# Six more tasks of a gelu stage moved into attention's last unit, and one relu half's additions moved behind its last tile

## What is computed

```python
x = x + 0.5 * gelu_mixture(layernorm(x))      # a: 8 experts, 128 -> 512 -> 128, the best 2 by router
x = x + attention(layernorm(x))               # b: 16 heads of 8, causal, rotary positions
x = x + 0.5 * gelu_mixture(layernorm(x))      # c: as a
x = x + 0.5 * relu_mixture(layernorm(x))      # d: 8 experts, 128 -> 256 -> 128, the best 1 by router
x = x + selective_scan(layernorm(x))          # e: 64 states, chunks of 64 steps
x = x + 0.5 * relu_mixture(layernorm(x))      # f: as d
```

## Time and profile before

| | us |
|---|---|
| median of 3 runs | 1462.83 |
| lowest and highest of them | 1460.21, 1464.10 |
| the profiled execution's own time | 1457.12 |
| its span, first to last instruction | 1455.0 |
| around the span | 2.12 |
| mean granted clock of PE over the span | 0.866 of full |
| busy in the span: PE, DVE, ACT, POOL | 1125.1, 971.6, 771.4, 747.8 |

### The profile page before, as it was taken

The page is one execution under the profiler, slowest core; times in us unless marked ns, Lnnn a source line. Parts: engine busy times, 40 slices in busy tenths (PEclk is TensorE's granted clock), DMA queues, the critical chain, the costliest instruction groups (busy, mean ns, idle before and its releaser), DMA issues.

```text
span 1455.0 us, 26867 instructions
## 1 busy us (share of the span) xinstructions
PE 1125.1 (77%) x9744; PEld 715.4 (49%) x9744; DVE 971.6 (67%) x2128; ACT 771.4 (53%) x1515; POOL 747.8 (51%) x658
## 2 busy tenths in 40 slices
PE   2869999758888888778899978816578888885784
PEld 1646767402222222355677655613466666664463
DVE  5887676677777777288766663355468888886332
ACT  2666667404666566667667733315655666651231
POOL 4774566573333331167466563525167888882322
PEclk9999999957999999889999988957578989985796
DMA  6110000031111120010000001210411111101122
GB/s 204 58 44 1 1 1 1 0 58 30 30 30 30 30 30 1 1 58 31 29 1 1 0 12 55 72 36 15 154 47 39 39 36 35 41 19 61 55 79 62
DMA packets 90601, 55.39 MB, mean 38 GB/s; under 512 B 54236, under 2 KB 83684, under 8 KB 89575
## 3 DMA queue, kind: packets, MB, share of 16 engines
q1 hardware_dynamic: 88423, 49.48, 12.9%
q0 software_dynamic: 2048, 4.20, 1.0%
HBM read 31.06 MB, written 14.20 MB: 31 GB/s over the span
## 4 chain that ended last, share of the span: by engine, by line
PE 42%; DVE 23%; issue 14%; ACT 13%; POOL 3%; SPq 2%; DMA 2%; POOLq 0%; DVEq 0%; ACTq 0%
PE ps L700 13%; PE ps L841 4%; PE ps L871 4%; DVE arena L1858 4%; PE ps L982 4%; DVE xn L1642 2%; ACT hr L1149 2%; PE ps L954 2%; DVE maxima L1861 2%; ACT arena L1249 2%; DVE arena L1929 2%; ACT arena L1149 2%; PE ps L809 2%; PE ps L793 2%; PE ps L769 1%
## 5 line engine op out<-in xcount | busy, mean ns | idle before, releaser
L1529 POOL TENSOR_TENSOR arena<-arena 128x512 f32<-128x512 f32 x126 | 214.8, 1724 | 86.4 <-ACT arena L1249 37.2
L700 PE MATMUL ps<-xp,wup 128*128 128x512 f32 x768 | 206.8, 415 | 13.1 <-ACT hr L1149 9.6
L1553 POOL TENSOR_TENSOR hr<-arena,hr 128x512 fp32r<-128x512 f32 x128 | 171.8, 1348 | 85.9 <-ACT hr L1149 85.9
L700 PE MATMUL ps<-hr,wdn 128*128 128x512 f32 x768 | 200.4, 411 | 3.8 <-issue 2.7
L1249 ACT ACTIVATE arena<-ps 128x512 f32<-128x512 f32 x256 | 143.2, 597 | 107.5 <-PE ps L954 101.4
L1149 ACT ACTIVATE arena<-ps 128x512 f32<-128x512 f32 x256 | 163.4, 638 | 61.7 <-PE ps L700 61.4
L1205 ACT ACTIVATE arena<-ps 128x1024 f32<-128x1024 f32 (+1 forms) x192 | 148.3, 810 | 79.6 <-PE ps L856 78.3
L1794 DVE TENSOR_TENSOR hr<-arena,hr 128x512 fp32r<-128x512 f32 x128 | 126.2, 997 | 87.8 <-ACT hr L1149 86.8
L700 PEld LDWEIGHTS ps<-xp,wup 128*128 128x128 f32 x768 | 146.5, 198 | 62.5 <-POOL wup L1540 16.8
L1929 DVE TENSOR_TENSOR arena<-arena,ps 128x1024 f32<-128x1024 f32 x189 | 154.1, 856 | 17.2 <-PE ps L967 16.9
L1149 ACT ACTIVATE hr<-ps 128x512 fp32r<-128x512 f32 x256 | 165.5, 646 | 0.0
(11 more groups left out here) (240 smaller groups left out, 1876.6 us busy)
## 6 DMA issues: line engine op xcount, KB each, us to landing
arena<-up_dram SPq DMA_DIRECT2D x16, 256.0 KB, 2.9
arena<-dn_dram SPq DMA_DIRECT2D x16, 256.0 KB, 3.1
ys_rows<-arena SPq DMA_DIRECT2D x8, 320.0 KB, 2.5
arena<-up_dram SPq DMA_DIRECT2D x2, 1024.0 KB, 4.8
arena<-dn_dram SPq DMA_DIRECT2D x2, 1024.0 KB, 6.9
arena<-xs_rows SPq DMA_DIRECT2D x4, 512.0 KB, 4.8
b_parts<-arena SPq DMA_DIRECT2D x1, 1536.0 KB, 5.0
dt_parts<-arena SPq DMA_DIRECT2D x1, 1536.0 KB, 6.4
```

The lines of the kernel that those rows point to most:

```text
L700: mm = e.matmul(out, left(a), right(b), start=(first and n == 0), stop=(last and n == 2))
L1529: e.tensor_tensor(hsf[t % 3][:, cols], decayf[u % 2][:, t4 * W + cols.start:t4 * W + cols.stop], hsf[(t - 1) % 3][:, cols], ALU.mult).then ...
L1553: e.tensor_tensor(hr[:, ex % 2, 1, fc, :], hid[:, ex % 2, fc, :], hr[:, ex % 2, 0, fc, :], ALU.subtract).then_inc(MX["rest_pool"], 1)
```

## The change

It does three things.

1. `early_tasks` grows from 3 tasks to 9: besides `stats` 0, `norm` 0 and `stats` 1 it now has `turn` 0, `logits` 0, `logits back` 0, `shift` 0, `norm` 1 and `route` 0 of stage c. They stand in the last unit ahead of steps 5 (`stats` 0, `norm` 0), 6 (`turn` 0), 7 (`logits` 0, `stats` 1), 8 (`logits back` 0), 9 (`shift` 0), 10 (`norm` 1) and 11 (`route` 0). Before stage c's first expert only `stats` 2 is left.
2. These tasks use PSUM banks 0 and 1 in the place of 6 and 7, with waits for the projection's additions (`proj_added`) and for the last split of heads (`unit_split`), and the projection of block 2 waits for the shift (`shifted`). `rot` moves to the end of attention's pieces, so that `xp` lies on it and not on pieces that the last unit still uses.
3. In the relu stages all 8 additions of the first half, and in stage d the scan's tasks behind them, go to the last step of the loop, s = 32.

```diff
--- before.py
+++ after.py
@@ -206,8 +206,6 @@
         qkf = carve(NT * 2 * D)
         qk = qkf.rearrange("p (i c d) -> p i c d", c=2, d=D)
         probT = qkf.rearrange("p (s h q) -> p s h q", s=2, h=HG)
-        rot = carve(2 * T + P)
-        rotv = rot[:, 0:2 * T].rearrange("p (c i d) -> p c i d", c=2, d=D)
         vflat = carve(T + P)
         vall = vflat[:, 0:T].rearrange("p (i d) -> p i d", d=D)
         ctxv = xn[:]
@@ -223,6 +221,8 @@
         masked_s = [qzf[:, n * S + 4 * P:n * S + 8 * P] for n in (2, 3)]
         vpad = carve(2 * ST_ * HG * 32).rearrange("p (s i h c) -> p s i h c", s=2, i=ST_, h=HG)
         oT = carve(2 * 512).rearrange("p (a q) -> p a q", a=2)
+        rot = carve(2 * T + P)
+        rotv = rot[:, 0:2 * T].rearrange("p (c i d) -> p c i d", c=2, d=D)
         assert top[0] <= kept
 
         top[0] = 0
@@ -367,9 +367,9 @@
                 before = [t(w, g) for g in range(NTB // B) for w in tasks_of(st)] + [t(w, 0) for w in ROUTED] + \
                          [t(w, g) for g in range(NTB // B, NTB) for w in tasks_of(st)] + [t(w, 1) for w in ROUTED]
             along = {5: [t("rweights", 0), t("rweights", 1)]}
-            along.update({NTL + 11 + n: [t("add", 2 * n), t("add", 2 * n + 1)] for n in range(HT // 2)})
+            along[B * NTL + 2] = [t("add", n) for n in range(HT)]
             if nxt:
-                along.update({NTL + 11 + HT // 2 + n: [(nxt, w, g) for w in tasks_of(nxt)] for n, g in enumerate(range(NTB // B))})
+                along[B * NTL + 2] += [(nxt, w, g) for g in range(NTB // B) for w in tasks_of(nxt)]
             return before, along
 
         AT = {k: sem(f"att_{k}") for k in (
@@ -437,11 +437,17 @@
 
         EARLY = NTB - NTB // B
         after = [stages[n + 1] for n, st in enumerate(stages[:-1]) if st["kind"] == "attention"]
-        early_tasks = [(after[0], "stats", 0), (after[0], "norm", 0), (after[0], "stats", 1)] if after else []
+        early_tasks = [(after[0], w, g) for w, g in (
+            ("stats", 0), ("norm", 0), ("turn", 0), ("logits", 0), ("stats", 1), ("logits back", 0), ("shift", 0),
+            ("norm", 1), ("route", 0))] if after else []
+
+        def task_bank(st, what, g):
+
+            return (0 if what == "turn" else 1) if (st, what, g) in early_tasks else (6 if what == "turn" else 7)
 
         def last():
             extra = {1: [("ctx", 0, 0)], 2: [("ctx", 0, 1), ("proj", 0, 0)], 3: [("proj", 0, 1)],
-                     **{5 + n: [("task", 0, n)] for n in range(len(early_tasks))}}
+                     **{4 + n: [("task", 0, k) for k in m] for n, m in enumerate(((0, 1), (2,), (3, 4), (5,), (6,), (7,), (8,)))}}
             m = -1
             for what, k, n in order(True, False):
                 if what == "st" and n % 2 == 0:
@@ -640,21 +646,25 @@
                 e.wait_ge(LN["xn_ready"], st["norm"] + g + 1)
                 if not (isinstance(n, int) and n == 0):
                     e.wait_ge(LN["xnT_ready"], n)
+                bank = task_bank(st, what, g)
+                if bank == 0:
+                    e.wait_ge(AT["proj_added"], NTB // B)
                 for j in range(TPB):
                     at = xn_flat[:, bass.ds(xn_at(st, g) + j * P, P)]
-                    mm = e.transpose(ps[:, 6, j * P:(j + 1) * P], at, ident[:])
+                    mm = e.transpose(ps[:, bank, j * P:(j + 1) * P], at, ident[:])
                 mm.then_inc(LN["tp_done"], 1)
             elif what == "logits":
                 n = st["route"] + g
                 e.wait_ge(LN["xnT_ready"], st["turn"] + g + 1)
                 if not (isinstance(n, int) and n == 0):
                     e.wait_ge(LN["shifted"], n)
-                e.matmul(ps[0:E, 7, :], rw[st["kind"]][:], xnT[:, bass.ts(g, TB)], start=True, stop=True
+                e.matmul(ps[0:E, task_bank(st, what, g), :], rw[st["kind"]][:], xnT[:, bass.ts(g, TB)], start=True, stop=True
                          ).then_inc(LN["logitsT_done"], 1)
             elif what == "logits back":
                 e.wait_ge(LN["logitsT_ready"], st["route"] + g + 1)
+                bank = task_bank(st, what, g)
                 for j in range(TPB):
-                    mm = e.matmul(ps[:, 7, j * E:(j + 1) * E], logitsT[:, j * P:(j + 1) * P], ident[0:E, 0:E],
+                    mm = e.matmul(ps[:, bank, j * E:(j + 1) * E], logitsT[:, j * P:(j + 1) * P], ident[0:E, 0:E],
                                   start=True, stop=True)
                 mm.then_inc(LN["logits_done"], 1)
             elif what == "rlogits":
@@ -922,6 +932,8 @@
             e.wait_ge(AT["o_normed"], 2 * NU + 2)
             for g in range(EARLY, NTB):
                 e.wait_ge(AT["proj_added"], g - 1)
+                if g == EARLY:
+                    e.wait_ge(LN["shifted"], after[0]["route"] + 1)
                 context(e, g)
             for g in range(EARLY, NTB):
                 project(e, g, 2 + g)
@@ -1116,12 +1128,15 @@
                 e.activation(std[:, 0:TPB], veps[:, 0:TPB], ACT.Sqrt).then_inc(LN["std_ready"], 1)
             elif what == "turn":
                 e.wait_ge(LN["tp_done"], st["turn"] + g + 1)
+                bank = task_bank(st, what, g)
+                if bank == 0:
+                    e.wait_ge(AT["unit_split"], 2 * NU)
                 if st["kind"] == 0:
-                    e.copy(xp[:, 0, bass.ts(g, TB)], ps[:, 6, :])
-                e.copy(xnT[:, bass.ts(g, TB)], ps[:, 6, :]).then_inc(LN["xnT_ready"], 1)
+                    e.copy(xp[:, 0, bass.ts(g, TB)], ps[:, bank, :])
+                e.copy(xnT[:, bass.ts(g, TB)], ps[:, bank, :]).then_inc(LN["xnT_ready"], 1)
             elif what == "logits":
                 e.wait_ge(LN["logitsT_done"], st["route"] + g + 1)
-                e.copy(logitsT[:], ps[0:E, 7, :]).then_inc(LN["logitsT_ready"], 1)
+                e.copy(logitsT[:], ps[0:E, task_bank(st, what, g), :]).then_inc(LN["logitsT_ready"], 1)
             elif what == "shift":
                 e.wait_ge(LN["shifted"], st["route"] + g + 1)
                 e.activation(lg[:], lg[:], ACT.Exp).then_inc(LN["exp_done"], 1)
@@ -1644,6 +1659,8 @@
                     ins.then_inc(LN["xn_ready"], 1)
                 elif what == "logits" and st["kind"] == 0:
 
+                    if task_bank(st, what, g) == 1:
+                        e.wait_ge(AT["unit_split"], 2 * NU)
                     e.wait_ge(LN["xnT_ready"], st["turn"] + g + 1)
                     cols = bass.ts(g, TB)
                     e.tensor_tensor(xp[:, 1, cols], xnT[:, cols], xp[:, 0, cols], ALU.subtract).then_inc(LN["rest_ready"], 1)
@@ -1652,7 +1669,7 @@
                     kind = st["kind"]
                     l = lg[:]
                     e.wait_ge(LN["logits_done"], st["route"] + g + 1)
-                    e.tensor_tensor(l, ps[:, 7, 0:TPB * E].rearrange("p (i e) -> p i e", e=E),
+                    e.tensor_tensor(l, ps[:, task_bank(st, what, g), 0:TPB * E].rearrange("p (i e) -> p i e", e=E),
                                     rb[kind][:].unsqueeze(1).to_broadcast([P, TPB, E]), ALU.add).then_inc(LN["route_step"], 1)
                     e.wait_ge(LN["route_step"], n + 1)
                     e.tensor_reduce(rowmax[:], l, AX.X, ALU.max).then_inc(LN["route_step"], 1)
```

## The result

| | before | changed |
|---|---|---|
| median of 15 runs, us | 1461.09 | 1449.08 |
| lowest and highest | 1456.82, 1477.89 | 1441.31, 1460.64 |
| profiled execution: its time, span | 1457.12, 1455.0 | 1449.86, 1448.1 |

The ratio of the times is **0.994, with a 95% interval of 0.9921 to 0.996**: faster by 0.6%, or 8.8 us (5.8 to 11.5). The forecast was a gain of 8.7 us, a median of 1454.1. The profiled executions differ by 7.3 us.

What follows compares the result with a forecast made beforehand. No single engine was taken to bound the span (PE 42% of the chain, DVE 23%). Gains of 4.4, 4.05 and 0.3 us sum to 8.7, so 1462.83 - 8.7 = 1454.1 us, range 1449.8 to 1460.2.

Steps and rivals of the forecast that it cites:

- Part 1a: Attention's last unit: the added copies and handovers lengthen it on ACT by 1.9 us, bounds 1.2 to 4.
- Part 1b: Start of stage c: no wait on `comb`, slow first up products, fast second; expert 2 starts 4.4 us earlier.
- rival B: PE keeps its clock over attention's closing transposes and projection: part 1 gives 6.5, 11 in all, 1451.8 us; chance 0.14.
- The late ranking costs twice: Stage c: PE waits 5.39 us for the split of `comb`, then expert 1's up products take 5.33, not 3.02.
- Part 2: End of stage d: the loop's last two steps take 2.88 us in place of 6.93, a gain of 4.05.
- Part 3: First half's additions leave the relu loops: a gain of 0.2 us in stage d and 0.1 in f.
- The 2.19 at f's end: Stage f's moved additions lie under 13.48 idle us; without that cover they would cost 2.19 us.
- Rival D: Reordered code brings new stalls of mean 4.9 us at three places: 6.0 us slower, 1468.8 us; chance 0.04.
- The median of the runs is 5.71 above that execution: Base of the forecast: 1462.83 us for the kernel before, against its profiled execution of 1457.12.

Runs made afterwards that it cites:

- attn_only: The changed kernel with the relu lines put back, so the attention part alone; ratio to the kernel before 0.9968.
- relu_only: The kernel before with only the relu stages' additions and scan tasks moved to the loop's last step; ratio to the kernel before 0.9958.
- the second pair: The kernel before and the changed kernel, both unedited, profiled again on the third group's chip; ratio of the changed one 0.9956, of the kernel before 1.0018.
- first pair: The kernel before and the changed kernel as first measured and profiled; ratio 0.994.
- gather_late: The changed kernel with POOL's gather of the first half held back until 21 tile results are copied, in both relu loops; ratio to the kernel before 0.9964.
- zero_late: The changed kernel with the relu tasks in their old places and POOL's 13.77-us memset behind the second gather; ratio to the kernel before 1.0044.
- before_hold: The kernel before with 28 filler products on PE in its wait for the split of `comb` in stage c; ratio to the kernel before 1.0011.
- rank_late: The changed kernel with the ranking (`route` 0) back before stage c's first expert; ratio to the kernel before 0.9946.
- adds_in_loop: The changed kernel with the first half's additions back in both relu loops, the scan's tasks staying at the last step; ratio to the kernel before 0.9926.
- after_again: The changed kernel, unedited, profiled again on the third group's chip; ratio to the kernel before 0.9956.

## Why the prediction was right

- *Part 1a, +1.9 on the unit.* Measured +2.03, within the bounds of 1.2 to 4. Of the profiles that begin the unit at 587 to 590 us, both of the kernel before have 25.14, and all five with the new attention 27.11 to 27.17; of the late ones attn_only has 28.36 and relu_only 26.50, which is +1.86. The +3.00 of the second pair crosses the two groups. The closing reciprocal was foreseen at 614.4; it came at 616.07, of which 1.51 is the late start.
- *Part 1b, -4.4.* The right mechanism, of the wrong size. Between like executions it is -6.2 (first pair), -5.4 (gather_late and zero_late against before) and -6.4 (attn_only against relu_only); the -4.2 of the second pair crosses the groups. Each landmark stands as predicted: half clock in the first group (5.33 foreseen, 5.11), no wait on `comb`, full clock in the second (2.98). The term that was mis-sized in the first pair is the passage from the reciprocal to expert 2: 638.3 - 614.4 = 23.9 foreseen, 22.00 measured. I took the transposes and the projection at their old length (6.0 us from the reciprocal); they took 5.0, with part of the 16 products at full clock. POOL's weight rest took 1.26 and not 1.63. And the second group followed the first by 5.53 us where I had 6.6: the transposes of `comb` and `turn` 1 took 0.6 together (630.26 to 630.85) and not 1.3. The full clock at 620 to 622 is rival B in a small form, which I had given 0.14. It is worth some 0.8 of the 1.9 (22.00 against the 22.8 of gather_late and zero_late, whose projection ran at half clock); the other 1.1 come with the earlier second group.
- *The late ranking costs twice.* Right in kind, wrong in weight. before_hold shows the second cost, the slow group, to be 1.07 us and too little to see in the time; rank_late puts ranking at 3.7 in all, more of it through expert 1's weights (1.52 us behind POOL, and a slow group of 4.61 us behind that) than through the wait on `comb` (0.41).
- *Part 2, -4.05.* Measured -4.5 and -4.4, with the step lengths as read off stage f (1.44) and 4.41 us of cover (4.2 foreseen). relu_only shows it alone. On chips without a standstill it is worth 4.8 to 7.1 (loop d of 84.20 in before_hold and 86.45 in attn_only against relu_only's 79.37), since there the old order meets the memset, as the last section shows; no row of before showed that.
- *Part 3, -0.3.* Nothing in d, at most 0.8 in f by adds_in_loop, and that within what kernels with the additions differ by. The 2.19 at f's end stayed hidden (11.29 idle us left).
- *Rival D.* No profile has a further standstill; the two there are moved by one step at most. The Trainium skill (Runtime: NRT & Kernel Launch, section Instruction fetch mechanics) says that code is fetched in sequence and the fetch hidden behind the rate of issue; that no reordering of the code here brought a new standstill agrees with it. The standstills at s = 21 and 22 it leaves unexplained.
- *The number.* 8.7 us forecast, 8.8 measured by the ratio. That they agree to a tenth is luck: the interval is 5.8 to 11.5, the landmarks of the two parts add up to 10.7 against a forecast of 8.45 for them, and 2.3 of these are gone again in stretches that no edit touches, or in f's loop. The median of 1449.08 lies 0.7 under the range. The step that failed is not a term of the sum but its base: "The median of the runs is 5.71 above that execution" took one offset for both kernels. In the 15 runs of each it was 3.97 for before and -0.78 for the change.

## What to carry to other kernels

Work that opens a stage is cheapest where an engine stands idle inside the stage before, and its price there is what it adds to the engine that is the bound (here 2 us of ACT against 8 in the passage). Before pricing a moved task, lay each small DVE operation of it beside POOL's long instructions: one of 13.77 us made a step of 3.5 us one of 7. And a slow group behind an idle stretch of PE need not be on the chain; ask what its consumers would do with it sooner.

## What the runs showed that was not expected

**A tiny DVE operation waits for POOL's whole instruction.** Timeline of attn_only, POOL and DVE:

```profile
941.60 13.77 POOL L1595 MEMSET arena<- 128x16384 bf16 x1
```

```profile
950.30 0.86 DVE L1632 BATCH_NORM_STATS2 stats<-x 128x6 f32<-128x128 f32 x4
951.30 0.38 DVE L1637 BATCH_NORM_AGGREGATE mv<-stats 128x2 f32<-128x6 f32 x4
951.71 3.68 DVE L1640 TENSOR_SCALAR veps<-mv 128x4 f32<-128x4 f32 x1
...
957.28 0.87 DVE L1632 BATCH_NORM_STATS2 stats<-x 128x6 f32<-128x128 f32 x4
958.30 0.38 DVE L1637 BATCH_NORM_AGGREGATE mv<-stats 128x2 f32<-128x6 f32 x4
958.71 0.17 DVE L1640 TENSOR_SCALAR veps<-mv 128x4 f32<-128x4 f32 x1
```

The same operation of 128x4 takes 3.68 us beside the memset and 0.17 behind it. It ends at 955.39, the memset at 955.37. So it is elsewhere: in zero_late, as shown above, at 981.36, the memset at 981.33; in gather_late at 946.97 + 4.98 = 951.95, memset 951.93; in before_hold, where it takes 1.71 us, at 950.73, memset 950.71; in the changed kernel it takes 1.27 at 625.21 and ends at 626.48, POOL's weight rest at 626.45. The statistics beside the same memset keep their 0.86 and 0.38. That the operation is held until POOL's instruction ends is what five ends within 0.03 us show, and no profile has an exception: wherever this operation begins while POOL is at work, it ends with an instruction of POOL. The Trainium skill (SBUF — State Buffer, section SBUF: two separate sides) says that DVE and GpSimd share a pair of ports as an exclusive lock, held for the whole instruction, which a DVE operation takes in a mode that uses two ports, or with two inputs in SBUF against a GpSimd operation that reads SBUF; the length of the hold agrees. Which mode an operation ran in no row here tells. ACT, which has the root of this result to take, stood for 4.11 us, and the loop with it. With the changed order the operation stands behind the loop, and in none of these profiles but gather_late's does it meet the memset.

**The time before the edit moves by 9 us with the clock.** The same kernel reaches attention's last unit, ahead of all edits, at different times in different executions. Windows of 300 us ahead of it, of the changed kernel and of after_again:

```profile
280.00:580.00 300.00, 238.84 (x1584) 69.61 (x1582) 231.72 (x758) 157.97 (x229) 116.82 (x208) 0.85 0.17 29
```

```profile
280.00:580.00 300.00, 243.04 (x1536) 71.88 (x1534) 226.88 (x748) 154.57 (x221) 115.48 (x205) 0.80 0.17 29
```

In the first profile, at a granted clock of 0.85 of full, the last unit's first projection addition comes at 588.90, in after_again, at 0.80, at 597.75. All profiles fall in two groups, 587 to 590 and 597 to 602, and the 15 runs of the change in two as well (ten at 1441 to 1450 us with a mean granted clock of 0.868 to 0.879, five at 1457 to 1461 with 0.852 to 0.863). Why the clock is lower in some executions was not tried; that it is what makes them longer is read from the two going together. A median here hangs on how many executions of either group it has, and the places of the change had to be read from landmarks within a profile, between profiles of one group.
